# Causal linear attention: running sums of 64-token blocks as quadrants of the TensorE array

## What is computed

```python
q = _feature_map(x @ wq + bq).reshape(b, t, H, D)   # x is the layer norm of the input
k = _feature_map(x @ wk + bk).reshape(b, t, H, D)   # where(x > 0, x + 1, exp(x))
v = (x @ wv + bv).reshape(b, t, H, D)
def step(carry, qkv):
    S = S + einsum('bhd,bhe->bhde', kt, vt)         # running sum over the tokens
    z = z + kt
    num = einsum('bhd,bhde->bhe', qt, S)
    den = einsum('bhd,bhd->bh', qt, z)[..., None] + EPS
    return ((S, z), num / den)
return out @ wo + bo
```

## Time and profile before

| | of the profiled execution |
|---|---|
| span | 631.7 us; the median of the runs is 631.92 us |
| PE busy | 575.6 us (91%), 3838 instructions |
| PEld busy | 442.8 us (70%) |
| DVE busy | 517.9 us (82%), 1602 instructions |
| ACT busy | 420.2 us (67%) |
| POOL busy | 427.0 us (68%) |
| granted TensorE clock | 1.00 in the attention loop, 0.982 over the span |

### The profile page before, as it was taken

One profiled execution on the slowest core, in us unless ns is written; L12 is line 12 of the kernel. 1 busy time (PEld: TensorE's weight loads), 2 busy tenths in 40 slices (PEclk: granted clock), 3 DMA queues, 4 the chain that ended last, 5 costly groups with the idle time before them and its releaser, 6 DMA issues.

```text
span 631.7 us, 15833 instructions
## 1 busy us (share of the span) xinstructions
PE 575.6 (91%) x3838; PEld 442.8 (70%) x3839; DVE 517.9 (82%) x1602; ACT 420.2 (67%) x1188; POOL 427.0 (68%) x461
## 2 busy tenths in 40 slices
PE   3899999999999999968799877999999999999993
PEld 1455555555555555545689644799999999989993
DVE  5599999999999999983678888566877887877883
ACT  3557777877787777351788512345788888878882
POOL 2899989998999899310877600765467666757762
PEclk9999999999999999999999968899999999999998
DMA  5610111111161111283477551221012111111110
GB/s 147 184 51 0 35 33 35 34 33 33 33 100 33 34 33 34 66 119 90 119 208 202 113 113 29 53 51 46 27 49 54 48 47 47 51 38 51 51 44 23
DMA packets 49973, 40.92 MB, mean 65 GB/s; under 512 B 21971, under 2 KB 40278, under 8 KB 49926
## 3 DMA queue, kind: packets, MB, share of 16 engines
q1 hardware_dynamic: 44150, 29.61, 19.0%
q0 software_dynamic: 4960, 10.49, 6.4%
q10 hardware_dynamic: 816, 0.26, 0.2%
HBM read 27.47 MB, written 12.88 MB: 64 GB/s over the span
## 4 chain that ended last, share of the span: by engine, by line
PE 63%; ACT 12%; DVE 12%; issue 6%; DMA 4%; POOL 1%; DVEq 0%; ACTq 0%; SPq 0%; POOLq 0%
PE bank L1329 57%; PE bank L1333 4%; ACT xh L671 3%; ACT xs L773 2%; PE bank L1568 2%; DMA w_s<-gram_d 1%; DVE on L935 1%; ACT ex L647 1%; ACT nb_c L668 1%; DVE mean_early L1037 1%; DMA circ<-prob_d 1%; PE bank L1492 1%; ACT rl L648 1%; ACT xrT L759 1%; ACT ex L653 1%
## 5 line engine op out<-in xcount | busy, mean ns | idle before, releaser
L542 POOL TENSOR_TENSOR shared<-v,qk 128x1152 f32<-128x1152 f32 x64 | 142.8, 2231 | 2.8
L1329 PE MATMUL bank<-shared,tri_s 128*128 128x360 f32 (+1 forms) x384 | 137.2, 494 | 0.7 <-DVE R L896 0.7
L609 POOL DMA_INDIRECT shared<-xs_d,row_u x91 | 87.8, 964 | 62.2 <-DVE row_u L1227 31.6
L896 DVE TENSOR_TENSOR R<-bank,qk 128x360 f32<-128x360 f32 (+1 forms) x192 | 96.2, 540 | 8.6 <-PE bank L1329 6.7
L1329 PEld LDWEIGHTS bank<-shared,tri_s 128*128 128x128 f32 x384 | 69.8, 192 | 44.9 <-issue 20.4
L616 POOL DMA_INDIRECT out_x<-shared x64 | 63.6, 993 | 48.4 <-DVE shared L1299 21.8
L905 DVE TENSOR_REDUCE nd<-R 128x144 f32<-128x1152 f32 x64 | 86.1, 1346 | 1.6
L1329 PE MATMUL bank<-w_s,hid 128*128 (+1 forms) x620 | 82.3, 276 | 0.1
L1329 PEld LDWEIGHTS bank<-w_s,hid 128*128 128x128 f32 x620 | 75.5, 192 | 0.6 <-issue 0.3
L812 ACT ACTIVATE shared<-bank 128x256 f32<-128x256 f32 x155 | 59.4, 384 | 21.9 <-PE bank L1329 16.2
L1320 DVE TENSOR_TENSOR hid<-bank,shared 128x256 f32<-128x256 f32 x155 | 61.4, 422 | 10.0 <-ACT shared L812 9.8
(11 more groups left out here) (247 smaller groups left out, 1138.4 us busy)
## 6 DMA issues: line engine op xcount, KB each, us to landing
xs_d<-xs SPq DMA_DIRECT2D x16, 270.0 KB, 4.7
X<-in_x SPq DMA_DIRECT2D x16, 256.0 KB, 2.8
ct<-in_ctx_t SPq DMA_DIRECT2D x16, 256.0 KB, 2.8
ct<-in_ctx_r SPq DMA_DIRECT2D x16, 256.0 KB, 3.6
gram_d<-gd SPq DMA_DIRECT2D x14, 256.0 KB, 2.4
w_s<-in_w_experts SPq DMA_DIRECT2D x8, 384.0 KB, 4.0
circ<-prob_d SPq DMA_DIRECT2D x30, 64.0 KB, 2.7
shared<-xs_d,row_u POOLq DMA_INDIRECT x91, 2.6
```

Source lines behind the costliest of these rows:

```text
L542: nc.gpsimd.tensor_tensor(outer[k], v9[k % 2][:].unsqueeze(3).broadcast_to([P, H, D1, D]), kk.unsqueeze(2).broadcast_to([P, H, D1, D]), AL ...
L609: nc.gpsimd.indirect_dma_start(xg[q], None, xs_d[:, :], bass.IndirectOffsetOnAxis(ap=rows, axis=0)).then_inc(xg_in[q], 16)
L896: nc.vector.tensor_tensor(R[:, lo:hi], bank[2 + c][:, 0:n_h * D1 * D].rearrange("p (h e d) -> p h e d", h=n_h, e=D1), qq.unsqueeze(2).broa ...
L1329: return nc.tensor.matmul(o, l, r, start=start, stop=stop, skip_group_check=True)
```

## The change

The outer products lose the constant 1: 16 heads x 8 x 8 = 1024 columns. The running sums of a tile become four matmuls of 64 x 64 weights (a diagonal block of `tri_s`) and 512 columns, one for each pair of a row half and a column half of the array. Columns 0 to 511 (heads 0 to 7) go from tokens 0 to 63 to partitions 0 to 63 and from 64 to 127 to 64 to 127; columns 512 to 1023 go crosswise. For that, k and v of heads 8 to 15 are projected with the two blocks of 64 tokens exchanged: the columns of the projection are reordered on the host (v of heads 0 to 7, q, k, v of heads 8 to 15), the first 256 are one matmul and the last 128 two matmuls with 64 weight columns each. A pair of banks holds the 1024 sums of a tile, and there are two such pairs, used in turn. The sum z comes from `key_sums`, once a group: two matmuls of 256 columns over k of four tiles, the second with a matrix `tri_f` that exchanges the blocks back. VectorE multiplies the pair of banks with q in one instruction, sums 1024 to 128, and has two operations a group more, `key_dots` and `sum_dots`. The denominators are formed in the group's own slot, the inverses are written to bank 6. The transposes of `xh` use bank 5, the context product bank 4 (shared with `key_sums`), behind the second tile's sums.

```diff
-tri_s, stri_s, id_s = sb("tri_s", [P, P]), sb("stri_s", [P, P]), sb("id_s", [P, P])
+tris_s, stri_s, id_s = sb("tris_s", [P, 2 * P]), sb("stri_s", [P, P]), sb("id_s", [P, P])
+tri_s, tri_f = tris_s[:, 0:P], tris_s[:, P:2 * P]
...
-v9 = [sb(f"v9_{i}", [P, H, D1]) for i in range(2)]
+v8 = [sb(f"v8_{i}", [P, E]) for i in range(2)]
...
-shared = sb("shared", [P, GT * H * D1 * D])
+shared = sb("shared", [P, 9 * GT * E])
...
-outer = [shared[:, i * H * D1 * D:(i + 1) * H * D1 * D].rearrange("p (h e d) -> p h e d", h=H, e=D1)
-         for i in range(GT)]
-R = sb("R", [P, H, D1, D])
-nd = [sb(f"nd{i}", [P, GT, H, D1]) for i in range(2)]
-den, rden = sb("den", [P, GT * H]), sb("rden", [P, GT * H])
+outer = [shared[:, i * D * E:(i + 1) * D * E] for i in range(GT)]
+R = sb("R", [P, (D + 1) * E])
+num = [sb(f"num{i}", [P, GT, E]) for i in range(2)]
+zq = sb("zq", [P, GT * E])
+den = sb("den", [P, GT * H])
...
-bank = [ctx.enter_context(nc.psum_tensor(f"bank{i}", [P, 512], F32)) for i in range(8)]
+def psum(name, banks=1):
+    return ctx.enter_context(nc.psum_tensor(name, [P, banks * 512], F32))
+run = [psum("run0", 2), psum("run1", 2)]
+bank = [run[0][:, 0:512], psum("bank1"), run[1][:, 0:512], run[1][:, 512:1024], psum("bank4"), psum("bank5"),
+        psum("bank6"), run[0][:, 512:1024]]
+rden = bank[6][:, 0:GT * H]
...
-        need(pool, b_mul, 3 * (t - 2 * GT) + 3)
+        need(pool, b_mul, t - 2 * GT + 1)
+        need(pool, b_dots, 2 * (g - 1) - 1)
...
-        need(pool, b_run, 3 * (t - GT) + 3)
+        need(pool, b_run, t - GT + 1)
...
+        vv = v8[k % 2][:].rearrange("p (h e) -> p h e", h=H)
...
-            outer[k], v9[k % 2][:].unsqueeze(3).broadcast_to([P, H, D1, D]),
-            kk.unsqueeze(2).broadcast_to([P, H, D1, D]), ALU.mult).then_inc(a_outer, 1)
+            outer[k].rearrange("p (h e d) -> p h e d", h=H, e=D), vv.unsqueeze(3).broadcast_to([P, H, D, D]),
+            kk.unsqueeze(2).broadcast_to([P, H, D, D]), ALU.mult).then_inc(a_outer, 1)
     def slot(n, i):
...
 def _(act):
+    v_halves = bass.AP(bank[1][:].tensor, 0, [[512, P], [HALF + 2 * E, 2], [1, HALF]])
     def a_evac_xT(g, p, r):
...
-        nc.scalar.activation(xT[:], bank[0][:], ACT.Copy).then_inc(a_xT, 1)
+        nc.scalar.activation(xT[:], bank[5][:], ACT.Copy).then_inc(a_xT, 1)
     def a_evac_proj(g, p, r, k):
...
-        nc.scalar.activation(v9[k % 2][:, :, 0:D], bank[1][:, 2 * E:3 * E].rearrange("p (h d) -> p h d", h=H),
-                             ACT.Copy).then_inc(a_pev, 1)
+        nc.scalar.activation(v8[k % 2][:].rearrange("p (c x) -> p c x", c=2), v_halves, ACT.Copy).then_inc(a_pev, 1)
...
     def denominators(g, p, r):
-        act.wait_ge(b_red, GT * g + GT)
-        need(act, c_rden, g)
-        nc.scalar.activation(den[:], nd[p][:, :, :, D].rearrange("p t h -> p (t h)"), ACT.Copy, bias=ATT_EPS).then_inc(c_den, 1)
+        act.wait_ge(b_dots, 2 * g + 2)
+        nc.scalar.activation(den[:], den[:], ACT.Copy, bias=ATT_EPS).then_inc(c_den, 1)
     def negative_mean(g, p, mv, mv_sem, mr, mr_sem):
...
     def slot(n, i):
-        a0, a1, c, d = (stage(n, i, s) for s in (2, 1, -1, -2))
+        a0, a1, b, c, d = (stage(n, i, s) for s in (2, 1, 0, -1, -2))
...
-        if c:
-            denominators(*c)
...
-            nc.scalar.activation(k2T[:], bank[7][:], ACT.Identity, bias=wkk[:, E:E + 1]).then_inc(d_kT, 1)
+            nc.scalar.activation(k2T[:], bank[4][:], ACT.Identity, bias=wkk[:, E:E + 1]).then_inc(d_kT, 1)
...
+        if b:
+            denominators(*b)
...
-    def times_q(g, p, r, k, pieces):
+    def times_q(g, p, r, k):
...
-        if pieces[0] == 0:
-            need(dve, b_red, t)
-        for c in pieces:
-            lo, hi = HEADS[c]
-            n_h = hi - lo
-            dve.wait_ge(b_run, 3 * t + c + 1)
-            qq = qk[p][:, k, lo * D:hi * D].rearrange("p (h d) -> p h d", h=n_h)
-            nc.vector.tensor_tensor(
-                R[:, lo:hi], bank[2 + c][:, 0:n_h * D1 * D].rearrange("p (h e d) -> p h e d", h=n_h, e=D1),
-                qq.unsqueeze(2).broadcast_to([P, n_h, D1, D]), ALU.mult).then_inc(b_mul, 1)
+        need(dve, b_red, t)
+        dve.wait_ge(b_run, t + 1)
+        qq = qk[p][:, k, 0:E].rearrange("p (h d) -> p h d", h=H)
+        nc.vector.tensor_tensor(
+            R[:, 0:D * E].rearrange("p (h e d) -> p h e d", h=H, e=D),
+            run[k % 2][:].rearrange("p (h e d) -> p h e d", h=H, e=D),
+            qq.unsqueeze(2).broadcast_to([P, H, D, D]), ALU.mult).then_inc(b_mul, 1)
     def sum_heads(g, p, r, k):
...
-        dve.wait_ge(b_mul, 3 * t + 3)
+        dve.wait_ge(b_mul, t + 1)
...
-        nc.vector.tensor_reduce(nd[p][:, k], R[:], AX.X, ALU.add).then_inc(b_red, 1)
+        nc.vector.tensor_reduce(num[p][:, k, :], R[:, 0:D * E].rearrange("p (x d) -> p x d", d=D), AX.X, ALU.add
+                                ).then_inc(b_red, 1)
+    def key_dots(g, p, r):
+        dve.wait_ge(b_keys, g + 1)
+        nc.vector.tensor_tensor(
+            zq[:].rearrange("p (k c x) -> p c k x", k=GT, c=2), bank[4][:].rearrange("p (c k x) -> p c k x", c=2, k=GT),
+            qk[p][:, :, 0:E].rearrange("p k (c x) -> p c k x", c=2), ALU.mult).then_inc(b_dots, 1)
+    def sum_dots(g, p, r):
+        dve.wait_ge(b_dots, 2 * g + 1)
+        need(dve, c_rden, g)
+        nc.vector.tensor_reduce(den[:], zq[:].rearrange("p (x d) -> p x d", d=D), AX.X, ALU.add).then_inc(b_dots, 1)
     def split_fold():
...
     def inverses(g, p, r):
...
-        need(dve, c_on, g)
-        nc.vector.reciprocal(rden[:], den[:]).then_inc(c_rden, 1)
+        need(dve, d_gd, g - 1)
+        need(dve, c_x1, g)
+        nc.vector.reciprocal(rden, den[:]).then_inc(c_rden, 1)
     def quotients(g, p, r):
...
+        dve.wait_ge(b_red, GT * g + GT)
...
-            on[:].rearrange("p t (h d) -> p (t h) d", h=H), nd[p][:, :, :, 0:D].rearrange("p t h d -> p (t h) d"),
-            rden[:].unsqueeze(2).broadcast_to([P, GT * H, D]), ALU.mult).then_inc(c_on, 1)
+            on[:].rearrange("p t (h d) -> p (t h) d", h=H), num[p][:].rearrange("p t (h d) -> p (t h) d", h=H),
+            rden.unsqueeze(2).broadcast_to([P, GT * H, D]), ALU.mult).then_inc(c_on, 1)
     def add_attention(g, p, r):
...
     def slot(n, i):
...
-            times_q(*b, 0, (0, 1, 2))
-        if b:
+            times_q(*b, 0)
...
-            times_q(*b, 1, (0,))
+            times_q(*b, 1)
...
-            times_q(*b, 1, (1, 2))
+            key_dots(*b)
...
+            sum_dots(*b)
...
-            times_q(*b, 3, (0,))
+            times_q(*b, 3)
...
-            times_q(*b, 3, (1, 2))
...
     def running_sums(g, p, r, k):
...
-        for c, (lo, hi) in enumerate(HEADS):
-            need(pe, b_mul, 3 * (t - 1) + c + 1)
-            mm(bank[2 + c][:, 0:(hi - lo) * D1 * D], tri_s[:], outer[k][:, lo:hi].rearrange("p h e d -> p (h e d)")
-               ).then_inc(b_run, 1)
+        need(pe, b_mul, t - 1)
+        settle(pe)
+        for c in range(2):
+            for row in range(2):
+                own, to = slice(row * L, row * L + L), (row + c) % 2 * L
+                last = mm(run[k % 2][to:to + L, c * 512:c * 512 + 512], tri_s[own, own],
+                          outer[k][own, c * 512:c * 512 + 512])
+        last.then_inc(b_run, 1)
+    def key_sums(g, p, r):
+        pe.wait_ge(a_f, GT * g + GT)
+        need(pe, b_dots, 2 * g - 1)
+        need(pe, d_kT, g - 2)
+        mm(bank[4][:, 0:GT * HALF], tri_s, qk[p][:, :, E:E + HALF])
+        mm(bank[4][:, GT * HALF:2 * GT * HALF], tri_f, qk[p][:, :, E + HALF:2 * E]).then_inc(b_keys, 1)
     def project(g, p, r, k):
...
-        mm(bank[1][:, 0:3 * E], xT[:, k * P:(k + 1) * P], wqkv[:]).then_inc(a_proj, 1)
+        mm(bank[1][:, 0:2 * E], xT[:, k * P:(k + 1) * P], wqkv[:, 0:2 * E])
+        for h in range(2):
+            last = mm(bank[1][h * L:h * L + L, 2 * E:3 * E], xT[:, k * P + (1 - h) * L:k * P + (1 - h) * L + L],
+                      wqkv[:, 2 * E:3 * E])
+        last.then_inc(a_proj, 1)
     def keep_warm(of, times):
...
+            pe.wait_ge(b_dots, 2 * NG - 1)
...
-            transposes(bank[0], xh).then_inc(a_tr, 1)
+            need(pe, d_xT, a1[0] - 3)
+            transposes(bank[5], xh).then_inc(a_tr, 1)
...
-        if d:
-            g, p, r = d
-            pe.wait_ge(ct_in[p], 16 * r + 16)
-            need(pe, d_kT, g)
-            if i is None and g == 0:
-                pe.wait_ge(kk_w, 1)
-            mm(bank[7][:], wkk[:, 0:E], ct[p][:]).then_inc(d_k, 1)
+        if b:
+            key_sums(*b)
...
+            if a1:
+                pe.wait_ge(a_xT, a1[0] + 1)
...
+        if d:
+            g, p, r = d
+            pe.wait_ge(ct_in[p], 16 * r + 16)
+            need(pe, d_kT, g)
+            if i is None:
+                need(pe, b_dots, 2 * min(g + 2, NG - 1) + 1)
+            else:
+                pe.wait_ge(b_dots, 2 * (g + 2) + 1)
+            if i is None and g == 0:
+                pe.wait_ge(kk_w, 1)
...
```

(42 more changed lines are left out.)

21 lines of the change are left out of this document (10 added, 11 removed).

## The result

The changed kernel takes 626.23 us (median of 8 runs, 623.75 to 631.28). The kernel before took 633.2 us on the same chip (8 runs, 631.75 to 634.38). The ratio is 0.9892, with a 95% interval from 0.9868 to 0.9917: 1.1% faster. The forecast was 619, with an own range of 608 to 628. The side and the case (A) were right; the gain was 7.0 us of 13.

What follows compares the result with a forecast made beforehand. TensorE, VectorE and GpSimd were nearly equally busy, so each engine's sum bounds the kernel. Fourteen slots of 14.6 us (-11.6) plus gains in the first two and last slots make -13: 631.9 to 619 us, own range 608 to 628, wider range 608 to 660.

Steps and rivals of the forecast that it cites:

- case (A): Whole kernel: the main forecast, 619 us, own range 608 to 628, a tile's sums under 1.0 us; chance 0.61.
- VectorE, 14.33 us a slot: Attention loop: merged multiplications and smaller head sum, less two added operations, take VectorE's work from 14.74 to 14.33 us.
- The quotients, 3.5 us of 14 slots: VectorE: with inverses read from PSUM, stalls against GpSimd's outer product vanish; three long slots in 14 cost 3.5 us.
- GpSimd, 12.9 us: Attention loop: outer products of 1024 instead of 1152 columns take GpSimd from 14.34 to about 12.9 us a slot.
- Sums, 1.03 us a tile: TensorE: four pairs of records on four quadrants, 0.058 us apart, each 0.85 long; 1.03 us instead of 1.94.
- B: TensorE's sums: the high record holds the queue, 2.15 us a tile, +46 us, 678 us; chance 0.14.
- D: TensorE's sums: row halves writing the same bank exclude each other, 2.6 us a tile, +71, 703 us; chance 0.04.
- TensorE, 14.2 us with 0.3 of waits: Attention loop, a slot: 9.8 us without sums, 4.1 of sums, 0.3 of waits; just under VectorE's 14.6.
- VectorE asks for 14.6 us a slot: Attention loop: VectorE's 14.33 us plus 0.2 to 0.3 idle set the slot; 14 slots give -11.6 us.
- The first two slots gain some 0.5 each: Start of the attention loop: the first two slots each get some 0.5 us shorter.
- The last slot some 0.5, nothing behind: End of the attention loop: the last slot gains some 0.5 us; nothing behind the loop changes.
- E: Attention loop: quadrants work, but mode changes and new waits leave TensorE at 15.2 to 15.5 us a slot, 628 to 636; chance 0.08.

Runs made afterwards that it cites:

- x4: Changed kernel with the inverses of the denominators written to SBUF again instead of bank 6: 629.9 us, 0.9962 of the kernel before.
- x5: Changed kernel without the exchange of blocks: both column halves on the same two quadrants, projections whole, `tri_s` for both key sums: 640.89 us, 1.014 of the kernel before.
- x1: Changed kernel with the context matmul behind the output projection instead of ahead of it: 627.67 us, 0.9906 of the kernel before.
- x8: Changed kernel with TensorE's transposes of the attention output ahead of the second tile's projection: 627.0 us, 0.9906 of the kernel before.
- x11: Changed kernel with transposes of `on` first, context matmul behind output projection, GpSimd's outer product ahead of variance, filling matmuls: 619.58 us, 0.9787 of the kernel before.
- x2: Changed kernel with GpSimd's first outer product of a group ahead of the variance of the next: 623.88 us, 0.9864 of the kernel before.
- x3: Changed kernel with unused filling matmuls where TensorE waits in slots 0, 1 and 15: 622.79 us, 0.9851 of the kernel before.
- x12: x11 with sums, key sums and projections over the whole array and no exchange of blocks: 631.14 us, 0.9992 of the kernel before.

## Why the prediction was right or wrong

- **VectorE, 14.33 us a slot**: 14.29 measured over the eleven full slots. The multiplication took 1.21 us, the reduction 1.21, the added pair 0.69 and 0.68. Right.
- **The quotients, 3.5 us of 14 slots**: 3.1 by x4; all 16 now take 0.67 to 0.69. Right, cause included. One reading was off: the quotients of the earlier trace rows did not end with the outer product of the earlier trace rows but 0.5 us behind it (149.99 and 149.44). They waited for its end and did their work then.
- **GpSimd, 12.9 us**: 12.99. Right.
- **Sums, 1.03 us a tile**: 1.02 with the change of mode in it. The picture was wrong: not four pairs 0.058 us apart, but four first records within 0.03 us, and the four second ones together 0.44 us later. That the size is right is partly luck: of the forecast's 1.03, 0.17 were for the spacing of pairs, which is not there; the 0.16 us that stand above 2 x 0.43 are around the change of mode, which the forecast had added elsewhere. With x5, a pair of gram records in the earlier trace rows is most likely one record on each half, not low and high of one half, so the conclusion from it, that a record waiting for its own half waits aside, was not shown. Of cases B and D there is no sign. The strict order that the Trainium skill states ("TensorE: Matmul & The Clock Gate", Part 3) could hold here only if the four low records are issued ahead of the four high ones; the trace does not tell which record is which (low and high are names for the two records here), so that stays open. For D the Trainium skill ("TensorEngine Tiling (Array Packing)", Gotcha 1) states that different row tiles cannot access the same PSUM bank simultaneously; here each bank got both row halves, on different partitions, within 0.03 us and with no delay, and the measurement decides.
- **TensorE, 14.2 us with 0.3 of waits**: 13.74 busy, 13.9 forecast. Right as a sum.
- **"VectorE asks for 14.6 us a slot"** is the first step that failed. It made the slot from the fullest engine plus an idle time carried over from before. The slot took 14.81 to 14.84, with VectorE idle for 0.55 and TensorE for 1.08 us, because of two rings: ScalarE and TensorE over the copy of `xT`, projections, key sums and transposes, and VectorE and TensorE over quotients, sums, context and addition. I had seen the first as waits in the earlier trace rows and priced only the work added on one engine. x1 and x8 took one ring each and won nothing; x11 took both and had 14.58. Of the 3.0 us missing in the 14 slots, 2.6 stand in the twelve steady ones; the late slot at half clock (15.23) has 0.6, and the first gave 0.2 back.
- **"The first two slots gain some 0.5 each"** is the second. They lost 2.3 us: the moments moved behind `sum_dots` on VectorE, GpSimd's variance waited 2.77 us for them, and with it the outer product, the copy of v and TensorE. I had asked what is queued behind the context matmul, and not what is queued behind the two added operations on VectorE and, through them, on GpSimd. In x2's trace one swap there gives back 2.8 us, part of it the clock's. The clock made it worse: 6.8 us at 1.2 GHz, and x3, which only keeps the clock, gives back 1.7. Price: 3.3 us. The late slot of 15.23 us instead of 13.79 (x3) is the clock's too, and counted above.
- **"The last slot some 0.5, nothing behind"**: 0.7 and 0.6. Right.
- **Case A or E?** The result lies at the upper end of A's own range (608 to 628), by E's kind of cause (new waits) at a smaller size than E had (slots of 15.2 to 15.5).

x11, at 619.58 us with 632.62 for the kernel before (0.9787; the forecast was 0.980), is where the forecast had put this kernel. It beats both the kernel before and the changed one.

## What to carry to other kernels

When the busy sums of three engines come within a few per cent, sum up rings as well: for each tile that passes from engine to engine and back within a period, add the work and the handovers along it, with what a change adds to them, and take the largest ring or sum. An edit that shortens one of two equal rings measures nothing; try the two together before dropping either. And for every operation added to an in-order queue, ask in the first iteration, too, what stands behind it and which other queue waits for that.

## What the hardware showed that I had not expected

- Eight records on four 64 x 64 quadrants: four start within 0.03 us and the four second ones together 0.44 us later, 1.02 us a tile. On two quadrants used twice (x5) a pair follows each 0.43 us, 1.86 us a tile.
- Cutting a matmul had its price: a projection of 256 columns and two of 128 on half the array took 1.0 us, the whole one 0.65 (x12, from 210.42 to 211.07 us).
- Much the same wait (1.56 and 1.57 us) stood just before a half-clock stretch in one kernel and before full clock in another (near 250 us in the changed kernel and x2).
- Quotients with both inputs in SBUF and GpSimd's outer product excluded each other whichever began first (x4: 2.45 or 2.44 us for the later one); with one input in PSUM they ran side by side (0.67 to 0.69 and 1.95 us).
